# First attention: raw scores from the high bf16 parts on two row groups, and half of the normalizing products moved to GpSimd

## The reference

```
# 1  first attention ("conv"): 4 heads, 32 channels a head
x = (input - mean) * scale + shift;  q, k, v = split(pw_w x)
attn = softmax(q.k / sqrt(32), axis=-1)     # over the 32 keys of ONE image row, not over all 1024
out = out_w (attn v) + out_b + input
# 2  causal attention over the 8 images' tokens (64 heads of size 2), RMS-normalized q and k
# 3  dense mixture of 8 experts, weighted by a softmax router
```

## Time and profile before

| | |
|---|---|
| time, median of 3 runs | 3805.63 us (3801.79 to 3808.67) |
| profiled execution | 3806.82 us, its span 3805.1 us |
| mean granted PE clock | 0.956 |
| first attention | from about 106 us to 958 us of the span |
| second attention | from about 1197 us to 3279 us of the span |

### The profile page before, as it was taken

One profiled execution on the slowest core, in us unless ns is written; L12 is line 12 of the kernel. 1 busy time (PEld: TensorE's weight loads), 2 busy tenths in 40 slices (PEclk: granted clock), 3 DMA queues, 4 the chain that ended last, 5 costly groups with the idle time before them and its releaser, 6 DMA issues.

```text
span 3805.1 us, 79261 instructions
## 1 busy us (share of the span) xinstructions
PE 3175.7 (83%) x27829; PEld 1180.1 (31%) x27829; DVE 1904.7 (50%) x2497; ACT 2817.5 (74%) x2759; POOL 300.4 (8%) x304
## 2 busy tenths in 40 slices
PE   5799999998773888888888888888888888779999
PEld 3344444444441222222222222222222222244443
DVE  3588878787575444444444444444444444452222
ACT  4444444444345999999999999999999999514555
POOL 5000000000354000000000000000000000001000
PEclk9899999999776999999999999999999999978999
DMA  5411111110143000000000000000000000200000
GB/s 186 115 40 47 48 44 47 48 32 10 38 144 124 17 16 17 17 17 17 17 17 17 17 16 16 16 17 17 17 17 17 17 17 16 72 17 6 11 14 14
DMA packets 118100, 134.09 MB, mean 35 GB/s; under 512 B 27246, under 2 KB 83660, under 8 KB 117964
## 3 DMA queue, kind: packets, MB, share of 16 engines
q1 hardware_dynamic: 117964, 132.29, 12.6%
HBM read 70.31 MB, written 55.57 MB: 33 GB/s over the span
## 4 chain that ended last, share of the span: by engine, by line
PE 57%; ACT 23%; issue 8%; DVE 5%; POOL 3%; SPq 1%; DMA 1%; ACTq 1%; DVEq 0%; POOLq 0%
ACT arena L878 22%; PE ps L1151 18%; PE ps L1128 10%; PE ps L989 3%; PE ps L1260 3%; PE ps L1267 3%; PE ps L1272 3%; PE ps L961 3%; PE ps L1007 2%; PE ps L1034 2%; PE ps L1009 2%; PE ps L1018 2%; DVE arena L1349 1%; POOL arena L698 1%; PE ps L1046 1%
## 5 line engine op out<-in xcount | busy, mean ns | idle before, releaser
L878 ACT ACTIVATE arena<-ps 128x1536 f32<-128x1536 f32 x1536 | 2063.8, 2095 | 11.0 <-PE ps L1128 11.0
L1151 PE MATMUL ps<-arena,Yall 128*32 128x512 f32 (+3 forms) x12288 | 1232.7, 496 | 10.8 <-POOL Yall L718 9.2
L1453 DVE TENSOR_TENSOR arena<-arena,causal 128x512 f32<-128x512 f32 x1024 | 674.3, 690 | 1043.4 <-ACT arena L878 1043.4
L1128 PE MATMUL ps<-Yall 15*128 15x512 bf16 (+3 forms) x6144 | 604.8, 330 | 396.7 <-ACT arena L878 373.8
L1128 PEld LDWEIGHTS ps<-Yall 15*128 15x128 bf16 x6144 | 163.2, 92 | 1277.3 <-ACT arena L878 1247.8
L803 ACT ACTIVATE arena<-ps 128x512 f32<-128x512 f32 x512 | 299.7, 595 | 293.3 <-PE ps L1009 283.8
L1151 PEld LDWEIGHTS ps<-arena,Yall 128*32 128x32 f32 x12288 | 284.1, 109 | 386.0 <-issue 360.4
L1349 DVE TENSOR_REDUCE arena<-ps 128x32 bf16<-128x1024 f32 x256 | 311.4, 1216 | 153.2 <-PE ps L989 153.2
L1356 DVE TENSOR_TENSOR arena<-arena,ps 128x512 f32<-128x512 f32 x512 | 329.2, 680 | 23.2 <-PE ps L1018 21.7
L1438 DVE COPY Yall<-ps 128x512 f32<-128x512 f32 x256 | 176.0, 688 | 198.3 <-PE ps L1151 198.3
L1009 PE MATMUL ps<-arena 128*128 128x256 bf16 x1024 | 257.5, 276 | 0.0
(11 more groups left out here) (172 smaller groups left out, 2083.8 us busy)
## 6 DMA issues: line engine op xcount, KB each, us to landing
Yall<-qstack SPq DMA_DIRECT2D x512, 30.0 KB
parts<-arena SPq DMA_DIRECT2D x8, 1536.0 KB, 5.9
arena<-parts SPq DMA_DIRECT2D x48, 256.0 KB, 5.4
arena<-parts SPq DMA_DIRECT2D x96, 128.0 KB, 2.8
Yall<-kstack SPq DMA_DIRECT2D x512, 24.0 KB
qstack<-arena SPq DMA_DIRECT2D x24, 384.0 KB, 3.2
attn<-Yall SPq DMA_DIRECT2D x512, 12.0 KB
arena<-arena SPq DMA_DIRECT2D x384, 16.0 KB, 1.8
```

What stands on the lines that cost most here:

```text
L878: act.activation(PR1[:, at:at + CW], bank(BPC * (kk % 2), BPC), ACT.Exp).then_inc(d_exp, 1)
L1128: mm = pe.matmul(bank(at + k)[:, s * P:(s + n) * P], Ks[par][HR * h:HR * h + QROWS, j * P:(j + 1) * P], Qs[par][HR * h:HR * h + QROWS, t * ...
L1151: mm = pe.matmul(o[HR * h:HR * (h + 1), :], Vg[par][:, j, 3 * h:3 * h + HR], pr[:, h * HALF + s * P:h * HALF + (s + n) * P], start=q < 2, ...
L1453: dve.tensor_tensor(v, v, m3, ALU.min).then_inc(d_mask, 1)
```

## The change

- Raw scores: in place of one head with 96 rows and all 1024 keys, a step takes two heads and 512 keys. Head n is read from rows 0 to 31 of `Q1` and `K1`, head n + 1 from rows 32 to 63 of `Q1` and `K2`; both hold high parts alone. The two products write banks 0 and 1. DVE's maximum has the same size, sorted otherwise into `maxima`.
- Normalizing: DVE keeps the product of heads 0 and 1. For heads 2 and 3 ACT copies the spread reciprocals from bank 5 into one half of the (still unused) tile `sel`, and POOL multiplies `E0` by them. The value product waits for both.
- On ACT the exponentials, and then the copy, stand ahead of the splits of the reciprocals (L792, L796 of before). POOL's low part is now ahead of POOL's product in step 4.
- `sel`, the constant that later stages need, is set by POOL after the first attention instead of at the program's start. PE waits for it (`f_set`) before the first product of the next stage.

```diff
@@ PE, raw scores
-                        par, q, qb, n = k // (TURN // 2), k // SUB % STEPS, k // NH0 % 2, k % NH0
+                        par, q, qb = k // (TURN // 2), k // SUB % STEPS, k // NH0 % 2
+                        n, th = k % NH0 // 2 * 2, k % 2
-                        for th in range(2):
-                            mm = pe.matmul(bank(th), Q1[q // 2][0:3 * D0, n, at:at + P],
-                                           half(K1[par][0:3 * D0, n, :], th), start=True, stop=True)
+                        for r, keys in enumerate((K1, K2)):
+                            mm = pe.matmul(bank(r), Q1[q // 2][D0 * r:D0 * (r + 1), n + r, at:at + P],
+                                           half(keys[par][D0 * r:D0 * (r + 1), n + r, :], th), start=True, stop=True)
@@ PE, spread and value product
-                            wait(pe, b_norm, K * 2 + (hp - 1 - 2 * L_NORM))
+                            wait(pe, (b_norm_low, b_copied)[hp], K - L_NORM)
-                        pe.wait_ge(b_norm, K * 2 + (2 - 2 * L_PV))
+                        pe.wait_ge(b_norm_low, K + (1 - L_PV))
+                        pe.wait_ge(b_norm_high, K + (1 - L_PV))
@@ ACT
+            def copy_spread(i, k, K):
+                if in_range(i, k, L_NORM):
+                    c = (k - L_NORM) % TURN
+                    act.wait_ge(b_spread_high, K + (1 - L_NORM))
+                    wait(act, b_norm_high, K + (-1 - L_NORM))
+                    act.activation(spread_c[c % 2], bank(5), ACT.Copy).then_inc(b_copied, 1)
@@ POOL
+            def pool_b(i, subs):
+                for k in subs:
+                    K = i * TURN + k
+                    if k % SUB == 4 and in_range(i, k, L_SUM + SUB + 2):
...
+                        pool.wait_ge(b_rmid, g + 1)
+                        wait_moved(pool, i, st - 1)
+                        pool.tensor_tensor(rec_parts[:, 2, :], rec_rest, rec_parts[:, 1, :],
+                                           ALU.subtract).then_inc(b_rlo, 1)
+                    if in_range(i, k, L_NORM):
+                        c = (k - L_NORM) % TURN
+                        e = E0[c // SUB % 2][:, c % SUB, 2:4, :].rearrange("p n q -> p (n q)")
+                        pool.wait_ge(b_copied, K + (1 - L_NORM))
+                        pool.tensor_tensor(e, e, spread_c[c % 2], ALU.mult).then_inc(b_norm_high, 1)
             pool.wait_ge(b_out, NSTEP)
+            pool.memset(sel[0:NE, :, :], 0.0).then_inc(f_set, 1)
+            pool.wait_ge(f_set, 1)
+            pool.affine_select(out=sel[0:NE, :, :], ... ).then_inc(f_set, 1)
@@ DVE
-                        for hp in range(2):
-                            e = E0[c // SUB % 2][:, c % SUB, 2 * hp:2 * hp + 2, :].rearrange("p n q -> p (n q)")
-                            dve.wait_ge(b_spread, K * 2 + (hp + 1 - 2 * L_NORM))
-                            dve.tensor_tensor(e, e, bank(4 + hp), ALU.mult).then_inc(b_norm, 1)
+                        e = E0[c // SUB % 2][:, c % SUB, 0:2, :].rearrange("p n q -> p (n q)")
+                        dve.wait_ge(b_spread_low, K + (1 - L_NORM))
+                        dve.tensor_tensor(e, e, bank(4), ALU.mult).then_inc(b_norm_low, 1)
```

More of the change, by code:

```diff
@@ L154, in hybrid_kernel @@
         sel = sb("sel", [P, NE, P])
+        flat_sel = sel[:, :, :].rearrange("p e c -> p (e c)")
         Yall = sb("Yall", [P, B, T])
@@ L203, in hybrid_kernel @@
         rec_parts = cut([3, QS], BF16)
-        maxima = cut([2 * NH0, GK], BF16)
+        maxima = cut([2, NH0, GK], BF16)
+        spread_c = [flat_sel[:, k * HALF:(k + 1) * HALF] for k in range(2)]
         spread = cut([NT, P], BF16)
@@ L300, in hybrid_kernel @@
         rs_loaded = [sem("rs_loaded_even"), sem("rs_loaded_odd")]
-        b_spread, b_norm, b_pv, b_out = [sem(n) for n in ("b_spread", "b_norm", "b_pv", "b_out")]
+        b_spread_low, b_spread_high = sem("b_spread_heads_01"), sem("b_spread_heads_23")
+        b_copied = sem("b_spread_heads_23_copied")
+        b_norm_low, b_norm_high = sem("b_norm_heads_01"), sem("b_norm_heads_23")
+        b_pv, b_out = sem("b_pv"), sem("b_out")
         c_pe, c_dve, c_act = [sem(n) for n in ("c_pe", "c_dve", "c_act")]
@@ L614, in _ @@
                                pattern=[[1, P]], channel_multiplier=-1).then_inc(ident_set, 1)
[L617 to L621, removed]
             pool.wait_ge(ident_set, 4)
@@ L657, in _ @@
                                            ALU.subtract).then_inc(a_lo, 1)
[L660 to L670, removed]
-            pool.wait_ge(b_out, NSTEP)
+            def pool_b(i, subs):
+                for k in subs:
+                    K = i * TURN + k
+                    if k % SUB == 4 and in_range(i, k, L_SUM + SUB + 2):
+                        st = (k - L_SUM - SUB - 2) // SUB
+                        g = i * (2 * STEPS) + st
+                        pool.wait_ge(b_rmid, g + 1)
[7 more added lines that the diff above has]
+                        pool.tensor_tensor(e, e, spread_c[c % 2], ALU.mult).then_inc(b_norm_high, 1)
+            turns(pool, pool_b)
+            pool.wait_ge(b_out, NSTEP)
+            pool.memset(sel[0:NE, :, :], 0.0).then_inc(f_set, 1)
+            pool.wait_ge(f_set, 1)
+            pool.affine_select(out=sel[0:NE, :, :], in_=sel[0:NE, :, :], compare_op=ALU.not_equal, fill=1.0,
+                               base=0, pattern=[[-1, NE], [0, P]], channel_multiplier=1).then_inc(f_set, 1)
+            pool.wait_ge(f_set, 2)
             pool.memset(V1, 1.0).then_inc(ones_set, 1)
@@ L787, in act_b @@
                         act.activation(sums, bank(7)[:, 0:QS], ACT.Copy).then_inc(b_summed, 1)
+                    if in_range(i, k, L_EXP):
+                        c = (k - L_EXP) % TURN
+                        for hp in range(2):
+                            act.wait_ge(b_qk, K * 2 + (hp + 1 - 2 * L_EXP))
+                            wait(act, b_pv, K + (1 - L_EXP - 2 * SUB))
+                            act.activation(E0[c // SUB % 2][:, c % SUB, 2 * hp:2 * hp + 2, :].rearrange("p n q -> p (n q)"),
+                                           bank(2 + hp), ACT.Exp, scale=SCALE0).then_inc(b_exp, 1)
+                            if hp == 1:
+                                copy_spread(i, k, K)
+                    else:
+                        copy_spread(i, k, K)
                     if k % SUB == 3 and in_range(i, k, L_SUM + SUB + 1):
@@ L976, in pe_b @@
                             mm = pe.matmul(bank(2)[3 * GK:P, n * P:(n + 1) * P],
-                                           maxima[:, (k + n - L_MOVE) % SUB, :], identb, start=True, stop=True)
+                                           maxima[:, (k - L_MOVE) // NH0 % 2, n, :], identb, start=True, stop=True)
                         mm.then_inc(b_moved, 1)
                     if in_range(i, k, 0):
-                        par, q, qb, n = k // (TURN // 2), k // SUB % STEPS, k // NH0 % 2, k % NH0
+                        par, q, qb = k // (TURN // 2), k // SUB % STEPS, k // NH0 % 2
+                        n, th = k % NH0 // 2 * 2, k % 2
                         if k % (TURN // 2) == 0:
@@ L1348, in dve_b @@
                         wait(dve, b_moved, i * (TURN // NH0) + (k // NH0 - 1))
-                        dve.reduce_max(maxima[:, k % SUB, :], bank(0, 2).rearrange("p (y x) -> p y x", x=GK), AX_X)\
-                            .then_inc(b_max, 1)
+                        n, y = k % NH0 // 2 * 2, k % 2 * (H // 2)
+                        dve.reduce_max(maxima[:, k // NH0 % 2, n:n + 2, y:y + H // 2],
+                                       bank(0, 2).rearrange("p (n y x) -> p n y x", n=2, x=GK), AX_X).then_inc(b_max, 1)
                     if in_range(i, k, L_NORM):
                         c = (k - L_NORM) % TURN
-                        for hp in range(2):
-                            e = E0[c // SUB % 2][:, c % SUB, 2 * hp:2 * hp + 2, :].rearrange("p n q -> p (n q)")
-                            dve.wait_ge(b_spread, K * 2 + (hp + 1 - 2 * L_NORM))
-                            dve.tensor_tensor(e, e, bank(4 + hp), ALU.mult).then_inc(b_norm, 1)
+                        e = E0[c // SUB % 2][:, c % SUB, 0:2, :].rearrange("p n q -> p (n q)")
+                        dve.wait_ge(b_spread_low, K + (1 - L_NORM))
+                        dve.tensor_tensor(e, e, bank(4), ALU.mult).then_inc(b_norm_low, 1)
                     if k % SUB == 2 and in_range(i, k, L_SUM + SUB):
```

8 lines of the change are left out of this document (1 added, 7 removed).

## The result

The changed kernel took 3829.11 us (median of 4 runs, 3825.67 to 3831.32), the kernel before 3807.15 us (4 runs). The ratio is 1.0059, with a 95% interval of 1.0041 to 1.0076: slower by 0.6%. The profiled execution has a span of 3826.3 us, 21.2 more than before, at a mean clock of 0.949. The forecast of 3823 and its direction held, but two thirds of the forecast rise were to come from a longer group of eight steps, and the group became shorter.

What follows compares the result with a forecast made beforehand. PE sets the pace, DVE close behind, with 1.3 us of slack in the RS chain. Terms +10.7 - 3.9 + 6 + 2.1 + 2.0 = +16.9 us gave 3823; own range 3814 to 3834 (chance 0.50).

Steps and rivals of the forecast that it cites:

- Raw scores: PE's raw-score pair on two row groups costs 0.22 instead of 0.44; 0.12 us won a step, 0.22 in steps 0 and 4.
- A: No drain between 32-row and 96-row products on PE: group 25.03, 3813 us; chance 0.15.
- D: The two row groups don't overlap, raw scores still cost 0.44 plus a drain: 3859 us; chance 0.06.
- ACT: Copy-out in step 0 moves back by 0.54, so PE's wait of 0.74 becomes 1.28; middle part ends at S(4) + 2.77.
- The RS chain: Later reciprocal parts delay SP's last eight moves, so step 7's spread comes at S(4) + 9.55 instead of 8.61.
- rival C: RS chain half as late, SP's issues at 0.62 instead of 0.69: group 24.8, 3806 us; chance 0.16.
- The term of +10.7 us: A group of eight steps takes 25.33 us against 24.96, +0.37, over 29 full groups.
- POOL: PE waits 0.6 to 0.8 for POOL's product behind the low part of step 4, covered by the RS wait.
- Lead-in and first chain: First nine steps win 3.9 us; the next ten win about 1.3, which the first RS chain takes back.
- Query loads: Loads behind the moves: PE waits 2.1, or 1.2 more, at five image starts: +6 us.
- Ends: Late middle part +1.5 and last eight steps +0.6 make +2.1; setting `sel` behind the first attention +2.0.
- Rival B: PE's win comes through, if ACT and SP keep up: group 24.04, 3779 us; chance 0.13.

Runs made afterwards that it cites:

- experiment 2: Changed kernel with ACT's high and middle parts of the reciprocals ahead of the exponentials again: 3787.52 us, ratio 0.9954 to the kernel before.
- experiment 6: Changed kernel with POOL's product ahead of the low part in step 4: 3831.0 us, ratio 1.0061 to the kernel before.
- experiment 3: Changed kernel with the six loads of the low query half ahead of the twelve moves into RS on SP: 3809.7 us, ratio 1.0008 to the kernel before.

## Why the prediction was right, and where it was not

The direction and the size were right (3823 forecast, 3829 measured), the split was not. By its steps:

- **Raw scores: right.** The pair stands 0.32 ahead of the scores: 0.22 of overlapped products and 0.10 that I put down to the change of tiling. By the Trainium skill, TensorEngine Tiling (Array Packing), Key Properties, a change of tiling mode drains TensorE; the trace agrees with that for 32 rows followed by 96, with these 0.10 us. The group of the raw half alone fell by 1.09; the term's 6 x 0.12 + 2 x 0.22 is 1.16. Rivals A (0.22 ahead) and D (0.5) are out.
- **ACT: right.** Middle part S(4) + 2.71 against 2.77, copy-out wait 1.23 against 1.28. S(3) to the turn 2.33, to S(4) 1.21, as worked out.
- **The RS chain, the step that decides: mis-sized.** "Eight moves, 8 x 0.69 = 5.5" was 4.95, at 0.62 a move, and S(4) + 9.55 was 9.02: I spread the one slow move over all twelve, and it mostly falls among the first four, where it costs nothing. So the group came to 24.77 and not 25.33, which is rival C's figure (24.8). The term of +10.7 us was -5.5 (29 x -0.19). The test that I set myself, "I am wrong if the spread of step 7 doesn't wait, or if the period is under 24.9", came out against me in both parts for the steady group; six spreads in all did wait for the moves, five of them near the start or the end.
- **POOL: right in size, wrong in weight.** PE reaches the product's end 0.63 late (S(4) + 4.83, against + 4.20 in experiment 2), inside my 0.6 to 0.8; its idle time in brackets is 0.45. I called it covered by the wait for RS; it is the one that shows, and the RS wait is what ends within 0.1 of it. "This one would be next" is what experiment 6 shows from the other side.
- **Lead-in and first chain: lead-in right, chain mis-sized.** 5.1 us were won by K = 20 (3.9 + 1.3 forecast); the first chain took back 5.0, not 1.3. PE waited 2.55 for it at 155.66 us (1.08 before), and the clock behind it was 0.50.
- **Query loads: wait right, price too low.** The raw scores wait 1.9 to 2.1, as forecast, but "1.2 more at the same five image starts: +6" priced only the wait. The starts and jumps lost 14.3. Behind the waits of 1.92 and 1.91 the clock fell, and the two groups lost 1.4 and 3.9 us more than those behind the waits of 2.06 and 2.00, where it stayed up.
- **Ends: mis-sized, the same way.** +2.1 forecast, 7.0 measured besides `sel`; from the last wait for `RS` to the attention's last product the mean clock was 0.61, where before had 0.82. `sel` cost 2.8 of wait (2.0 forecast), and 9 with what followed. The other end of that term, "At the program's start nobody waited for it", doesn't hold either: the stage begins 2.3 us earlier. The first raw product starts at 105.05 to 106.12 us in the four kernels that set `sel` at the start and at 103.31 to 104.45 in the nine that set it late; who waits for it there is not shown.

That the number came out is luck. Two errors of opposite sign cancelled: the group 16 us too dear, the first chain, the image starts and jumps and the end some 18 us too cheap (3.8, 8.3 and 5.7). The earlier start (-2.3) and the later stages (+4.8) were in no term. Rival C, with the right group, gave 3806, further off than mine; with these three places at their measured size it comes to about 3825. Rival B (3779) was wrong for this kernel, but its mechanism stands: with ACT's order mended the group is 24.03, where B had 24.04.

## What to carry to other kernels

Work moved to an idle engine is paid for by what stands behind it in that engine's order: here the half with the copies cost 48 us, though ACT had room for them, and putting two small instructions ahead of them gave 42 back. Price a wait at the edge of a loop by its length and, as a risk on top, by the clock behind it. Read a queue's issues one by one: a mean over a group spreads one slow issue over all, and where that one falls decides what it costs. When two waits end within a tenth of a microsecond of each other, look for their common cause; mending one alone showed nothing here.

## What the runs showed of the hardware

- POOL's float32 product of 128 x 512 took 1268 ns on average over 256 (page of after), the 1.26 of its quickest place before, while DVE did the same product from PSUM beside it in 678 ns:

```profile
L673 POOL TENSOR_TENSOR arena<-arena,sel 128x512 f32<-128x512 f32 x256 | 324.4, 1268 | 399.1 <-ACT sel L785 396.8
L1379 DVE TENSOR_TENSOR arena<-arena,ps 128x512 f32<-128x512 f32 x256 | 173.6, 678 | 48.7 <-PE ps L1040 47.8
```

- TensorE's granted clock fell behind some waits of about 2 us and not behind others of the same length at the same place of an image. In the changed kernel it stayed at 1.00 behind 2.06 and 2.00 us and fell (0.56 and 0.66 over the next 3 us) behind 1.92 and 1.91; behind the wait for the first chain it read 0.50 after 2.55 us, and 1.00 after 2.54 in experiment 3. The traces don't show what decides. At the end of the attention it stayed at 0.51 for 14 us, while PE was busy for 12.6 of them.
- A small move takes 0.62 to 0.63 us on SP's queue and PE starts on it 1.3 us behind the last one's end. In 29 of 32 groups of twelve before and in 22 after, one move takes 0.8 to 2.0 us, mostly the fifth to ninth in the kernel before and the second in the changed one; the traces don't show why. This one is the ninth of the group at 534.36 shown above:

```profile
539.41 1.54 SPq L478 DMA_DIRECT2D arena<-arena  x1
```
